# Key copies of six groups on POOL, one scaling of p on DVE, and the split of the expert weights at another place in an audio tower kernel

## The reference, cut to what matters

```
h = relu(sum over 8 taps f: window(x, f) * filt[f] @ W[f] + b)          # (32, 248, 64)
n = layernorm(h)
q, k, v = n @ Wq.T + bq, n @ Wk.T + bk, n @ Wv.T + bv
mask = (q[..., 0] != 0) & (k[..., 0] != 0)
prob = where(mask, softmax(q @ k.T / 8), 0)
h = h + (prob @ v) @ Wo.T + bo
n = layernorm(h)
top 2 of n @ Wg + bg + bias, softmax over the two -> combine            # 8 experts
y_e = relu(n @ W1[e] + b1[e]) @ W2[e] + b2[e]
h = h + sum over e: y_e * combine_e
```

## Time and profile before

| | us |
|---|---|
| median of 3 runs | 298.57 (297.52 to 299.38) |
| the profiled execution | 298.85 |
| its span in the profile | 297.1 |
| PE busy | 279.3 (94%) |
| DVE busy | 241.1 (81%) |
| ACT busy | 238.9 (80%) |
| POOL busy | 103.8 (35%) |

### The profile page before, as it was taken

How to read it: one execution, slowest core, us unless ns; L and a number is a source line. 1 busy time by engine, 2 the same in 40 slices (tenths; PEclk the granted TensorE clock), 3 DMA queues, 4 the chain that set the end, 5 groups by cost and what they waited for, 6 DMA issues and landing times.

```text
span 297.1 us, 6188 instructions
## 1 busy us (share of the span) xinstructions
PE 279.3 (94%) x1737; PEld 200.4 (67%) x1737; DVE 241.1 (81%) x890; ACT 238.9 (80%) x549; POOL 103.8 (35%) x99
## 2 busy tenths in 40 slices
PE   7776999999999999999999999999998999998993
PEld 6544657777777768677777777686776675665572
DVE  2576669989897979889898979798898899895666
ACT  3449598898998889898989989898887788876762
POOL 2204023442536162443415351715342151506051
PEclk9998899999999999999999999999999999999999
DMA  6430206061433526170624426250605133242301
GB/s 189 108 96 9 73 34 176 4 172 57 114 113 76 152 71 158 37 191 4 164 65 109 118 71 159 71 155 31 163 2 130 45 104 89 87 105 69 91 19 34
DMA packets 12785, 27.58 MB, mean 93 GB/s; under 512 B 3152, under 2 KB 5456, under 8 KB 12752
## 3 DMA queue, kind: packets, MB, share of 16 engines
q1 hardware_dynamic: 12464, 26.91, 33.8%
q10 hardware_dynamic: 288, 0.28, 0.3%
HBM read 20.85 MB, written 2.27 MB: 78 GB/s over the span
## 4 chain that ended last, share of the span: by engine, by line
PE 69%; DVE 12%; DMA 7%; issue 5%; ACT 4%; POOL 1%; POOLq 0%; SPq 0%; DVEq 0%; ACTq 0%
PE bank_y L1379 15%; PE bank_a L1290 11%; PE bank_h L1363 7%; PE bank_h L1364 7%; PE bank_s L1307 5%; PE bank_s L1419 4%; DMA kk<-kk 4%; PE bank_s L1318 4%; PE bank_s L1386 3%; DVE acc L820 3%; PE bank_b L1390 2%; PE bank_s L1390 2%; PE bank_s L1440 2%; PE bank_b L1386 2%; PE bank_b L1430 1%
## 5 line engine op out<-in xcount | busy, mean ns | idle before, releaser
L465 ACT ACTIVATE hid<-bank_h,col 128x496 f32<-128x496 f32 x128 | 84.3, 672 | 10.8 <-PE bank_h L1364 7.1
L374 POOL TENSOR_TENSOR p<-p,rmask 124x496 f32<-124x496 f32 x32 | 32.5, 1016 | 97.9 <-DVE rmask L863 97.7
L1379 PE MATMUL bank_y<-hid,w_sb 128*64 128x248 f32 x508 | 63.7, 380 | 0.8 <-DVE acc L820 0.7
L1363 PE MATMUL bank_h<-xs,w_hi 128*128 128x496 f32 x128 | 58.1, 454 | 0.2 <-DVE xs L256 0.2
L820 DVE SCALAR_TENSOR_TENSOR acc<-bank_y,col,cb 128x248 f32<-128x248 f32 x127 | 53.1, 468 | 4.7 <-PE bank_y L1379 1.9
L1364 PE MATMUL bank_h<-xs,w_lo 128*128 128x496 f32 x128 | 49.5, 387 | 0.0
L1379 PEld LDWEIGHTS bank_y<-hid,w_sb 128*64 128x64 f32 x508 | 32.8, 136 | 24.7 <-issue 11.2
L268 POOL TENSOR_TENSOR total<-acc 128x496 f32<-128x496 f32 x16 | 20.0, 1251 | 46.1 <-DVE acc L820 45.9
L456 ACT ACTIVATE p<-bank_s,nmax 124x248 f32<-124x248 f32 x64 | 29.3, 464 | 2.3 <-DVE nmax L852 1.1
L388 POOL TENSOR_TENSOR x_lo<-x,x_hi 128x512 fp32r<-128x512 f32 x16 | 20.6, 1291 | 24.9 <-ACT x_hi L524 24.9
L1363 PEld LDWEIGHTS bank_h<-xs,w_hi 128*128 128x128 f32 x128 | 24.1, 189 | 7.0 <-issue 3.6
(11 more groups left out here) (120 smaller groups left out, 545.8 us busy)
## 6 DMA issues: line engine op xcount, KB each, us to landing
cb<-weights SPq DMA_DIRECT2D x60, 248.0 KB, 3.9
kk<-kk SPq DMA_DIRECT2D x16, 248.0 KB, 3.0
x<-xt SPq DMA_DIRECT2D x15, 256.0 KB, 3.5
out<-h SPq DMA_DIRECT2D x16, 124.0 KB, 3.7
w_sb<-w SPq DMA_DIRECT2D x3, 256.0 KB, 4.0
wtok_sb<-wtok SPq DMA_DIRECT2D x1, 256.0 KB, 2.7
x<-xt ACTq DMA_DIRECT2D x1, 256.0 KB, 3.8
weights<-ct_sb SPq DMA_DIRECT2D x15, 15.5 KB, 1.4
```

Source lines behind the costliest of these rows:

```text
L374: pool.tensor_tensor(p_sb[b][0:HALF, :, :], p_sb[b][0:HALF, :, :], rmask[0:HALF, b, :].unsqueeze(2).to_broadcast([HALF, 2, WIN]), ALU.mult ...
L465: act.activation(hid[2 * (p % 2) + s][:, :], bank_h[s][:, 0:TOK], ACT.Relu, bias=col[:, C_B1 + e:C_B1 + e + 1]).then_inc(hid_ready[s], 1)
L1363: pe.matmul(bank_h[e % 2][:, 0:TOK], w1_hi[:, e, :], xs[m % 2][:, :], start=True, stop=False)
L1379: last = pe.matmul(dst[b * D:b * D + D, :], w2_sb[:, 2 * p + s, :], hid[2 * (p % 2) + s][:, b * WIN:(b + 1) * WIN], start=True, stop=True)
```

## The change

For groups 0 to 2 and 13 to 15 the keys are copied by two POOL instructions, `copy_high` (64x496, as soon as ACT has written the high part) and `copy_low` (64x496, after the low part), in place of SP's transfer; groups 3 to 12 keep the transfer. The scores of the six groups wait for the new semaphore `k_moved`. In POOL's list the copies of group 0 stand behind the low part of x for group 2, those of group 1 behind that for group 3, those of group 2 behind that for group 4, ahead of the first sum of group 0; those of groups 13, 14 and 15 stand behind the folds of groups 10, 11 and 12. The second p of group 0 is scaled by a new DVE step, `scale_first`, behind its `masked_recip`, ahead of the low tokens of group 1; PE's transpose of it waits for `p_first`, and all later counts of `p_ready` go down by one. On DVE, `expert_high` and `expert_low` move behind `both_taps(2)`, ahead of `residual(0)`.

```diff
@@ SP @@
             def fill():
                 load(2)
-                copy_keys(0)
                 load(3)
                 load(4)
-                copy_keys(1)
                 load(5)
                 store_weights(0)
                 spread(0, 0)
-                copy_keys(2)
                 spread(0, 1)
@@ drain: copy_keys(13), copy_keys(14), copy_keys(15) taken out in the same way @@
@@ POOL @@
+            def copy_high(n):
+                pool.wait_ge(kh_ready, n + 1)
+                after(pool, sc_done, 2 * n)
+                if n >= KEYS_TO:
+                    pool.wait_ge(k_copied, 16 * (KEYS_TO - KEYS_FROM))
+                if n < KEYS_FROM:
+                    pool.wait_ge(xl_ready, min(n + 3, 5))
+                else:
+                    pool.wait_ge(fold_ready, n - 2)
+                pool.tensor_copy(kk[0:D, 0, :], kk[D:128, 0, :].bitcast(F32)).then_inc(k_moved, 1)
+
+            def copy_low(n):
+                pool.wait_ge(kl_ready, n + 1)
+                pool.wait_ge(k_moved, moved(n) + 1)
+                pool.tensor_copy(kk[0:D, 1, :], kk[D:128, 1, :].bitcast(F32)).then_inc(k_moved, 1)
+                pool.wait_ge(k_moved, moved(n) + 2)
...
                 low_inputs(2)
+                copy_high(0)
+                copy_low(0)
                 scale(0, 0)
-                scale(0, 1)
                 low_inputs(3)
+                copy_high(1)
+                copy_low(1)
                 scale(1, 0)
                 scale(1, 1)
                 low_inputs(4)
+                copy_high(2)
+                copy_low(2)
                 add(pool, 0, 1)
                 scale(2, 0)
@@ DVE @@
+            def scale_first():
+                dve.wait_ge(rm_ready, 2)
+                dve.tensor_tensor(p_sb[1][0:HALF, :, :], p_sb[1][0:HALF, :, :],
+                                  rmask[0:HALF, 1, :].unsqueeze(2).to_broadcast([HALF, 2, WIN]),
+                                  ALU.mult).then_inc(p_first, 1)
...
                 low_keys(0)
-                expert_high()
                 low_queries(0)
                 keep_values(0)
                 masks(0)
-                expert_low()
                 rowmax(0, 0)
...
                 masked_recip(0, 1)
+                scale_first()
                 low_tokens(1, 0)
                 low_tokens(1, 1)
                 both_taps(2)
+                expert_high()
+                expert_low()
                 residual(0)
@@ PE @@
             def scores(n, b):
-                pe.wait_ge(k_copied, 16 * n + 16)
+                if KEYS_FROM <= n < KEYS_TO:
+                    pe.wait_ge(k_copied, 16 * (n - KEYS_FROM) + 16)
+                else:
+                    pe.wait_ge(k_moved, moved(n) + 2)
```

More of the change, by code:

```diff
@@ L191, in audio_tower @@
         k_copied = sem("k_copied")
+        k_moved = sem("k_moved")
+        p_first = sem("p_first")
         v_done = sem("v_done")
@@ L229, in audio_tower @@
         TOPK = 10
+        KEYS_FROM, KEYS_TO = 3, 13
         def after(eng, s, value):
@@ L257, in low_part, with moved @@
                                      ALU.subtract)
+        def moved(n):
+            return 2 * (n if n < KEYS_FROM else n - KEYS_TO + KEYS_FROM)
         def last_of_all(m, p):
@@ L342, in drain @@
                 spread(11, 0)
-                copy_keys(13)
                 spread(11, 1)
@@ L348, in drain @@
                 spread(12, 1)
-                copy_keys(14)
                 store_weights(13)
@@ L352, in drain @@
                 spread(13, 0)
-                copy_keys(15)
                 spread(13, 1)
@@ L417, in drain @@
                 fold_halves(10)
+                copy_high(13)
+                copy_low(13)
                 add(pool, 11, 1)
@@ L422, in drain @@
                 fold_halves(11)
+                copy_high(14)
+                copy_low(14)
                 add(pool, 12, 1)
@@ L427, in drain @@
                 fold_halves(12)
+                copy_high(15)
+                copy_low(15)
                 scale(15, 0)
@@ L856, in recip @@
                 dve.wait_ge(ex_ready, 2 * n + b + 1)
-                after(dve, p_ready, 2 * n + b - 1)
+                after(dve, p_ready, 1 if n == 1 else 2 * n + b - 2)
                 dve.reciprocal(rsum[0:HALF, b, :], psum_p[0:HALF, b, :]).then_inc(rs_ready, 1)
@@ L1312, in turn_p @@
             def turn_p(n, b):
-                pe.wait_ge(p_ready, 2 * n + b + 1)
+                if n == 0:
+                    pe.wait_ge((p_ready, p_first)[b], 1)
+                else:
+                    pe.wait_ge(p_ready, 2 * n + b)
                 for j in range(2):
```

## The result

The changed kernel takes 299.43 us (median of 22 runs, 298.29 to 301.32), the kernel before, timed beside it, 298.13 (22 runs, 296.72 to 299.38): a ratio of 1.0049 [1.0033, 1.0066]. It is 1.3 us slower by the medians, 1.5 us by the ratio, where 1.8 us less was forecast. Its profiled execution took 299.9 us, with a span of 297.7.

What follows compares the result with a forecast made beforehand. PE bounds the middle, so only fill and drain have slack. -1.0 (fill) and -0.76 (drain) make about -1.8 us: 297.05 from the profiled 298.85, median 296.8, chance 0.42, range 294.9 to 299.2.

Steps and rivals of the forecast that it cites:

- Bounds, the first step: From 60 to 230 us TensorE is busy 168.88 of 170 us, so only the ends have slack.
- I take it that nothing moves there: Between 60 and 230 us PE's busy share does not fall; a fall would make the forecast wrong.
- Part 1, keys and scores: Fill, group 0: POOL copies of 0.75 us each, PE's centring then leads, scores come 1.43 us earlier.
- rival (e): Fill: POOL's first copy must bring in its code; group 0's keys at 24.1, total +1.9 us, 300.5; chance 0.07.
- Part 2: Fill, group 0's second p scaled by DVE: ready 0.35 us earlier, alone worth 0.2 to 0.3 us.
- Part 3: Fill, moved split of expert weights: low half waits for POOL's low part of x, ends at 29.7; 1.0 us gained.
- Fill: 31.2 - 30.2 = 1.0 us gained: Fill: group 0's second centring, before at 31.21 us, comes at 30.2, a gain of 1.0 us.
- rival (b): Fill: DVE gets port before POOL, clock does not fall, group 15's mask not held; -3.3 us, 295.3; chance 0.07.
- The queues: SP's earlier loads gain nothing; on POOL, group 2's copies delay group 0's first sum 1.5 us, costed at nothing.
- the cover of group 2: Fill: PE still has group 0's products before it takes group 1's low tokens; failing costs at most 1.25 us.
- Part 4, the drain: Drain: PE's waits of 0.66 and 0.50 us in groups 13 and 14 go, group 15 loses 0.40; -0.76 us.
- a term that the forecast held at 1.75: Time around the span in the profiled execution: 1.75 us of 298.85, with a span of 297.1.

Runs made afterwards that it cites:

- e6_pad: The kernel before plus one useless DVE memset of 128x1 at the place of scale_first: 298.73 us, ratio 1.006.
- e4_group2: The changed kernel with group 2's keys copied by the transfer again: 298.45 us, ratio 1.0035.
- e13_split_early: Changed kernel, useless PE products in two holes; split's high part and half its low part ahead of first normalising, rest behind third taps: 298.05 us, 0.9998.
- filled pair: e9_before_busy and e10_after_busy, the kernel before and the changed kernel, each with useless PE products in holes of the fill: 297.09 and 298.70 us.
- e1_drain: The kernel before with only the keys of groups 13 to 15 copied by POOL: 297.99 us, ratio 0.9994.
- e10_after_busy: The changed kernel with useless PE products in two holes of the fill and 8 more ahead of group 0's second centring: 298.70 us, ratio 1.0013.
- e9_before_busy: The kernel before with useless PE products in two holes of the fill (6 and 5 of them): 297.09 us, ratio 0.9966.
- e5_nofirst: The changed kernel with the second p of group 0 scaled by POOL again, one DVE instruction fewer: 298.65 us, ratio 1.0036.
- e16_best_split: e17_best_again's kernel with the split's high part ahead of the first normalising and its low part behind the third sum of taps: 295.66 us, ratio 0.9942.
- e14_early_group2: e13_split_early with group 2's keys by a transfer as before: 297.43 us, ratio 0.9981.
- e15_early_pad: e14_early_group2 with one useless DVE memset of 128x1 more ahead of the first normalising: 297.47 us, ratio 0.9968.
- e17_best_again: Repeat: kernel before with POOL copying keys of groups 0, 1, 13, 14, 15, and useless PE products in two holes: 296.43 us, ratio 0.9982.

## Why the prediction was wrong

**Bounds, the first step: right in the main.** PE is busy 168.57 of 170 us in the middle. "I take it that nothing moves there" was wrong by 0.75 us in group 6.

**Part 1, keys and scores: right.** Copies of 0.60 us (0.75 forecast), the scores led by PE's centring, 1.54 us earlier (1.43 forecast). The first copy costs no more than the others: 0.60 at 18.19, so rival (e) did not happen. The Trainium skill's two rates for such a copy (GPSIMD Engine Reference, Performance versus the Vector engine and When to use GPSIMD) would give 0.74 and 0.41, both estimates; the trace lies between them.

**Part 2: right in size, wrong in price.** The scaling takes 0.68 us as forecast. That it adds an instruction to DVE I did not count as an effect at all; by e6_pad it costs 0.2 to 0.5 us in group 6.

**Part 3: the failed step is "Fill: 31.2 - 30.2 = 1.0 us gained".** The collision itself came as worked out: POOL first, the low half 2.18 us, the residual at 29.7 by my reckoning and at 29.70 net of the late start, the centring at 30.2 and at 30.22. So the 1.0 us was there, up to the centring, in this pair of executions. Two things made a gain out of it that was none. First, the base: I subtracted from a centring that stood at 31.21 only because PE ran at 0.52 of its clock in that execution. With the clock kept up the kernel before has its mark at 29.42, and 29.90 is a loss of 0.48. Second, the clock: the earlier trace rows had shown me that it falls after a slack stretch of PE, and I priced its staying up (rival (b)) but not its falling again. The changed kernel leaves PE a hole of 1.76 us, and in its profiled execution the fall comes behind it, on the chain: the logits of group 0 stand at 35.67, 0.57 later than before, though the residual was only 0.18 late. None of its 22 runs has the high mean clock that 65 of 147 runs of the kernel before have. That the fall lies behind this very hole is seen in one trace; in that of e4_group2 it lies from 26 to 31 us. e13_split_early shows the other side: without the collision the fill is 1.45 us shorter. I had worked out that the split would wait for POOL, but not that by this the change gives away all of its own gain.

**The queues: the cover of group 2 failed.** I had named the place and the price (up to 1.25 us) and costed it at nothing; it is 0.35 in the first profile, 0.28 in the filled pair.

**Part 4, the drain: right in the trace, too large as a mean.** From group 12 to 14 the marks gain 1.17 us (1.16 forecast). The mask of group 15 takes 0.59 instead of 0.16 and a loss of 0.24 follows (0.40 forecast). But the waits of 0.66 and 0.50 were those of one execution: the other four traces with the transfers have none for group 13 and 0.30 us in the mean for group 14. So more than half of the 1.16 was luck of the trace that I read: against the mean of five traces e1_drain gains 0.34 us from group 12 to 15, and at equal clock its runs are 0.5 to 0.6 us faster. In the filled pair the drain gives back 0.23 from group 12 to 14 and nothing in the end, but there e10_after_busy's residual of group 13 waits 0.36 us for an output transfer (out<-h), as it does not in the changed kernel.

Of the 1.71 us between the profiled executions of e9_before_busy and e10_after_busy, 0.48 is the fill's, 0.28 group 2's, 0.46 group 6's. The drain from group 12 to 15 is 0.0 in sum, and 0.4 lie outside the span (2.25 against 1.84 us). Those 0.4 are no chance of one execution. In all 22 runs of the changed kernel 2.17 to 2.36 us lie outside the span, in the 147 runs of the kernel before 1.75 to 1.95, in the mean 2.24 against 1.81: a third of the 1.3 us between the medians, and a term that the forecast held at 1.75. Taking back group 2's copies alone (e4_group2) gives a mean of 1.92, taking back scale_first alone (e5_nofirst) 1.87. What makes them stays open.

## What to carry to other kernels

Before a gap between two marks is counted as a gain, ask whether the earlier mark would stand there in another execution: look at the granted clock around it and at how long the same transfer takes elsewhere. When an operation with two SBUF inputs is moved on DVE, write down what POOL wants in that window, and place it where DVE asks first or where POOL is idle; e16_best_split has a fill 1.05 us shorter than e9_before_busy that way. An instruction added to a full engine can cost far from where it stands, so compare the marks of every group and not only of those that the change touches. And sort the runs of both kernels by their mean granted clock before comparing medians: here the two kinds of one kernel lie 1.6 us apart, more than the whole difference between the two kernels.

## What the runs showed of the hardware

- DVE is idle for 0.28 to 0.30 us near 120 us, with nothing to wait for that the profile shows where it stands ahead of the addition or the reciprocal. One instruction more ahead of it moved it by one instruction in e6_pad (weighing to addition) and from e14_early_group2 to e15_early_pad (addition to reciprocal); one behind it moved nothing. Where POOL's scaling starts in that moment, the addition takes 0.76 instead of 0.19 us.
- A POOL operation that waits for DVE is held as well: the copy of 0.60 us took 1.38, the low part of 1.27 took 1.92. In the collisions read here, who asked first went first.
- Short products of no use in PE's holes (11 of them, at 1.95 us for 8 some 2.7 us of PE time) kept the granted clock at 0.996 or more in all 12 runs of e9_before_busy, which lie within 0.86 us, at a ratio of 0.9966 [0.9944, 0.9988]; the 35 runs of the kernel before beside it spread over 4.07. They are no sure cure: 2 of 12 runs of e17_best_again have 0.991 and 0.994, two more take 298.3 us at 1.00 for a reason not seen here, and its runs spread over 3.10 us.
- The same transfer kk<-kk of 248 KB lands 3.0 to 4.8 us after its issue in the drain, over five traces.
